# First-round maxima of the last layer one iteration earlier, and the second layer's values-times-weights product as three f32r products

## Time and profile before

| | us |
|---|---|
| median of 3 runs | 2929.89 (2924.7 to 2931.28) |
| the profiled execution | 2927.05 |
| its span, first to last instruction | 2924.9 |
| PE busy | 2673.6 (91%), at a mean granted clock of 0.916 |
| DVE busy | 1857.2 (63%) |
| ACT busy | 1210.1 (41%) |
| POOL busy | 270.2 (9%) |

### The profile page before, as it was taken

The page is one execution under the profiler, slowest core; times in us unless marked ns, Lnnn a source line. Parts: engine busy times, 40 slices in busy tenths (PEclk is TensorE's granted clock), DMA queues, the critical chain, the costliest instruction groups (busy, mean ns, idle before and its releaser), DMA issues.

```text
span 2924.9 us, 25567 instructions
## 1 busy us (share of the span) xinstructions
PE 2673.6 (91%) x9636; PEld 1380.7 (47%) x9636; DVE 1857.2 (63%) x1973; ACT 1210.1 (41%) x2073; POOL 270.2 (9%) x138
## 2 busy tenths in 40 slices
PE   7999978989999898998989999898998989997888
PEld 4446644445544455444554445444464445542333
DVE  4624137776377764776558763787628777387987
ACT  3233122626235352444525354252632626224548
POOL 0030210010101001020110201002020010200000
PEclk7999987989989898998989989898998989978889
DMA  2000010100201011010200102001020100211100
GB/s 85 1 0 0 1 44 0 44 1 19 54 1 44 1 40 33 1 44 1 72 1 1 44 1 72 0 1 44 1 72 0 35 10 12 47 44 44 44 1 29
DMA packets 29292, 72.09 MB, mean 25 GB/s; under 512 B 10224, under 2 KB 10416, under 8 KB 28912
## 3 DMA queue, kind: packets, MB, share of 16 engines
q1 hardware_dynamic: 29168, 70.45, 9.6%
HBM read 11.40 MB, written 8.39 MB: 7 GB/s over the span
## 4 chain that ended last, share of the span: by engine, by line
PE 74%; DVE 18%; ACT 4%; issue 2%; SPq 1%; DMA 0%; DVEq 0%; ACTq 0%
PE ps L748 15%; PE ps L601 12%; PE ps L634 11%; PE ps L911 7%; PE ps L620 7%; DVE ba_nmx L1277 6%; PE ps L833 6%; PE ps L609 5%; DVE fa_nmx L1277 3%; PE ps L690 2%; PE ps L819 2%; ACT prb L1130 2%; DVE bb_nmx L1277 1%; DVE accb L1439 1%; PE ps L830 1%
## 5 line engine op out<-in xcount | busy, mean ns | idle before, releaser
L1130 ACT ACTIVATE prb<-ps 128x512 f32<-128x512 f32 x896 | 483.5, 601 | 319.4 <-PE ps L634 279.4
L1277 DVE TENSOR_REDUCE ba_nmx<-ps 128x1 f32<-128x1024 f32 x448 | 529.9, 1216 | 96.8 <-PE ps L620 94.4
L620 PE MATMUL ps<-ks,qs 96*128 96x512 f32 x896 | 374.6, 524 | 84.4 <-DVE ba_nmx L1277 64.1
L748 PE MATMUL ps<-pr,h 128*128 128x512 f32 x896 | 421.3, 595 | 1.6 <-ACT tmp L1029 1.0
L1439 DVE TENSOR_TENSOR accb<-accb,prb 128x1024 f32<-128x1024 f32 x336 | 394.0, 1217 | 14.8 <-ACT prb L1130 14.2
L634 PE MATMUL ps<-qs,ks 97*128 97x512 f32 x896 | 354.4, 471 | 13.9 <-ACT prb L1130 13.3
L1001 ACT ACTIVATE pr<-ps 128x512 f32<-128x512 f32 x336 | 195.5, 596 | 396.0 <-PE ps L833 188.6
L620 PEld LDWEIGHTS ps<-ks,qs 96*128 96x128 f32 x896 | 182.3, 227 | 266.3 <-DVE ba_nmx L1277 185.6
L634 PEld LDWEIGHTS ps<-qs,ks 97*128 97x128 f32 x896 | 161.6, 194 | 266.0 <-ACT prb L1130 201.0
L911 PE MATMUL ps<-prb,vb 128*32 128x512 f32 x1792 | 241.2, 611 | 2.9 <-ACT prb L1130 2.2
L748 PEld LDWEIGHTS ps<-pr,h 128*128 128x128 f32 x896 | 168.8, 190 | 148.6 <-issue 134.7
(11 more groups left out here) (300 smaller groups left out, 3058.9 us busy)
## 6 DMA issues: line engine op xcount, KB each, us to landing
qs<-part SPq DMA_DIRECT2D x168, 128.0 KB, 2.4
ks<-part SPq DMA_DIRECT2D x168, 128.0 KB, 2.4
xm<-in_x SPq DMA_DIRECT2D x8, 1024.0 KB, 5.7
out<-prb SPq DMA_DIRECT2D x28, 256.0 KB, 2.1
q2k<-part SPq DMA_DIRECT2D x48, 128.0 KB, 2.4
w<-in_weights SPq DMA_DIRECT2D x1, 2592.0 KB, 8.7
out<-pr SPq DMA_DIRECT2D x4, 256.0 KB, 2.0
qs<-ba_nmx_r SPq DMA_DIRECT2D x56, 4.0 KB, 1.8
```

The costliest lines, as they stand in the source:

```text
L620: mm = pe.matmul(o.ps[:, bank + jc, :], queries[0:STACK, tile(it)], keys[0:STACK, cols(jc)], start=True, stop=True)
L748: mm = pe.matmul(o.ps[:, 2 + ch, :], o.v[:, jt, tile(ch)], o.pr[:, t % 4, :], start=jt == 0, stop=jt == NT - 1)
L1130: act.activation(weights3(o, s, g), o.ps[:, turn3[score_use(s, g) % 3], :], ACT.Exp)\
L1277: dve.tensor_reduce(o.nmx[:, head, it:it + 1], o.ps[:, bank:bank + 2, :], AX.XY, ALU.max, negate=True).then_inc(o.max_sb[n].sem, 1)
```

## The change

Two things change, and all tables of `ORDER` are replaced.

1. **The head of a back is longer.** On PE it now reaches to the last of the 32 tiles of the first round's maxima, on DVE to the cast of these maxima, on SyncE to the four DMAs that write them into the queries. So the iteration that finishes batch b also takes the first-round maxima of batch b+1; for batch 0 they stand at the end of "fronts", and "backs" no longer has those of batch 6.
2. **Layer 1's product of values and weights is three f32r products.** ACT writes the values rounded to f32r (`v_hi`), DVE the rest (`v_lo`). Behind each of the 16 exponentials ACT copies the weights, rounded, to `p_hi`; POOL subtracts to get `p_lo`; PE sums `v_hi p_hi + v_hi p_lo + v_lo p_hi`. `p_hi` and `p_lo` have three buffers each. The product now waits for POOL's `p_lo`, and three steps instead of two lie between the scores and it.

```diff
@@ ORDER: all fifteen tables are replaced
...
+            o.v_hi, o.v_lo = tokens(o.ql2), tokens(o.kh2)
+            o.p_hi = [o.kl2[:, 0, 0:IW], o.kl2[:, 0, IW:], o.kl2[:, 1, 0:IW]]
+            o.p_lo = [o.kl2[:, 1, IW:], o.qh2[:, 1, 0:IW], o.qh2[:, 1, IW:]]
...
@@ sync
                         yield from stacks(b, u)
+                        yield from shift_rows(b, u)
                         if u == 0:
                             yield "head"
-                        yield from shift_rows(b, u)
...
@@ gpsimd
+                def low_part(b, t):
+
+                    pool.wait_ge(o.p_hi_sb.sem, o.p_hi_sb.at(b, t + 1))
+                    pool.tensor_tensor(o.p_lo[t % 3], o.pr[:, t % 4, :], bf32(o.p_hi[t % 3]), ALU.subtract)\
+                        .then_inc(o.p_lo_sb.sem, 1)
...
                         for jg in range(4):
+                            for t in (2 * (4 * ic + jg), 2 * (4 * ic + jg) + 1):
+                                if n == 1:
+                                    low_part(b, t)
+                                    yield
                             add_pair(b, n, 4 * ic + jg)
...
@@ tensor
-                        pe.wait_ge(o.exped[n].sem, o.exped[n].at(b, t + 1))
+                        if n == 1:
+                            pe.wait_ge(o.p_lo_sb.sem, o.p_lo_sb.at(b, t + 1))
+                        else:
+                            pe.wait_ge(o.exped[n].sem, o.exped[n].at(b, t + 1))
...
+                            for values, weights in ((o.v_hi, o.p_hi), (o.v_hi, o.p_lo), (o.v_lo, o.p_hi)):
+                                mm = pe.matmul(o.ps[:, 2 + ch, :], values[:, jt, tile(ch)], weights[t % 3],
...
+                    behind = 3 if n == 1 else 2
...
-                        yield "head" if half else None
+                        yield
...
-                            yield
+                            yield "head" if u == 0 and k == QUAD * NT - 1 else None
...
@@ scalar
+                        if n == 1:
+                            act.wait_ge(o.exped[1].sem, o.exped[1].at(b, t + 1))
+                            if t >= 3:
+                                act.wait_ge(o.weighed[1].sem, o.weighed[1].at(b, t - 2))
+                            act.activation(o.p_hi[t % 3], o.pr[:, t % 4, :], ACT.Copy).then_inc(o.p_hi_sb.sem, 1)
+                            yield
...
@@ vector
-                    yield "head"
+                    yield
...
-                        yield
+                        yield None if u else "head"
```

More of the change, by code:

```diff
@@ L762, in chunks @@
                         yield
-                        if t > 1:
-                            weigh(t - 2)
+                        if t >= behind:
+                            weigh(t - behind)
                             yield
@@ L768, in chunks @@
                             yield
-                    for t in (STEPS - 2, STEPS - 1):
+                    for t in range(STEPS - behind, STEPS):
                         weigh(t)
@@ L1033, in chunks @@
                         yield
-                        if t == NT + 1:
+                        if n == 1:
[4 more added lines that the diff above has]
+                            yield
+                        if t == (NT + 2 if n == 1 else NT + 1):
                             take(0)
@@ L1088, in front @@
                     yield from to_stacks(b, 1, True)
-                    take_values(b, 1, 0, o.v, 2)
-                    yield
+                    for half in range(2):
+                        act.wait_ge(o.v_ps[1].sem, o.v_ps[1].at(b, half + 1))
+                        act.activation(o.v_hi[:, 4 * half:4 * half + 4, :].rearrange("p (k a) c -> p k a c", a=2),
+                                       o.ps[:, 2 - 2 * half:4 - 2 * half, :].rearrange("p k (a c) -> p k a c", a=2),
+                                       ACT.Copy).then_inc(o.v_hi_sb.sem, 1)
+                        yield
                     shift_row(b, 1, o.qs01, ROW)
@@ L1399, in front @@
                     yield from low_stacks(b, 1, True)
-                    take_values(b, 1, 1, o.v, 0)
-                    yield
+                    for half in range(2):
+                        dve.wait_ge(o.v_hi_sb.sem, o.v_hi_sb.at(b, half + 1))
+                        rows = slice(4 * half, 4 * half + 4)
+                        dve.tensor_tensor(o.v_lo[:, rows, :].rearrange("p (k a) c -> p k a c", a=2),
+                                          o.ps[:, 2 - 2 * half:4 - 2 * half, :].rearrange("p k (a c) -> p k a c", a=2),
+                                          bf32(o.v_hi[:, rows, :]).rearrange("p (k a) c -> p k a c", a=2), ALU.subtract)\
+                            .then_inc(o.v_sb[1][half].sem, 1)
+                        yield
                     yield from maxima(b, 1, 1)
```

40 lines of the change are left out of this document (25 added, 15 removed), and 48 rows, old and new, of the table ORDER.

## The result

The changed kernel takes 2853.26 us (median of 4 runs, 2852.63 to 2854.85) against 2929.23 us for the kernel before on the same chip: a ratio of 0.9744, 95% interval 0.9727 to 0.9760. Forecast were 2731 us, with a range of 2630 to 2835. The direction was right, but three fifths of the expected 198 us didn't come. The profiled execution took 2852.89 us with a span of 2851.1.

A forecast was written before the change was run, and what follows sets the result against it. Iterations were taken to alternate between PE waiting for DVE and pure PE bound. Four stretches sum to 319.5 us; 469.7 + 6 x 319.5 + 339.4 = 2726 us of span, 2731 us forecast, range 2630 to 2835.

The forecast's parts named there:

- fronts: Part ahead of the six iterations: 435.9 us plus 39.1 for 32 uncovered tiles less 5.3 for shorter products, 469.7 us.
- backs: Part after the six iterations, DVE bound: 378.5 us less 39.1 for the maxima it no longer has, 339.4 us.
- What bounds the kernel: Middle iteration: stretches where PE waits for DVE alternate with pure PE ones; 57 of 351.6 us lost and winnable.
- Part 1: Layer 1's three f32r products: 5.3 us less PE work per batch, 42 us in all, real only where PE bounds.
- B: Layer 1's chunks with second-round maxima: PE 42.4, DVE 46, POOL 40.5 us, coupled; 48 us, bounds 44 and 56.
- The subtraction: POOL's 16 subtractions per batch in layer 1's chunks: 1.27 us each, 20.3 us per batch.
- POOL and DVE: Layer 1's chunks: POOL's additions and subtractions can delay four DVE pieces with SBUF inputs; 4 us allowed, range 0 to 9.
- A: Middle, first 16 steps and layer 0: 88.5 us of PE work times 1.11, the like old stretch's factor; 98.5 us.
- C: Second 16 steps and layer 2's projections: 74.3 us of work with a 6.6 us stall; 86 us, bounds 80 and 92.
- D: Layer 2's chunks, next head and its first-round maxima: 84.1 us of PE work, 87 us with 3 for the seam.
- the overlap: Head's first tile: its wait for 24 stack DMAs just hidden by 18.7 us of PE work; no-overlap rival 0.08.
- POOL becomes the bound: Rival for layer 1's chunks: subtractions of 2.0 us or waiting for DVE stall PE; 2765 to 2805 us, chance 0.15.

The follow-up runs named there:

- m1: Changed kernel with DVE's maxima of layers 0 and 1 read over 64 of 1024 columns; 2787.7 us.
- s1: Changed kernel with DVE's 32 second-round maxima of the last layer read over 64 of 1024 columns; 2791.9 us.
- m3: Changed kernel with all maxima, both rounds, read over 64 of 1024 columns, PE's products kept; 2675.7 us.
- h1: Changed kernel with layer 1's product as one f32 product per block, without ACT's copies and POOL's subtractions; 2858.8 us.
- n1: Changed kernel without POOL's subtractions: three products kept, rounded weights used twice, low parts of the weights left out; 2857.0 us.
- h2: Changed kernel with layer 1's product in f32, no low parts, and second-round maxima read over 64 of 1024 columns; 2812.1 us.
- m2: Changed kernel with the score products of layer 0's and 1's maxima computed twice into the same banks; 2848.1 us.
- c2: Changed kernel with seven unused PE products ahead of group norm 2, in the middle iterations alone; 2845.2 us.
- o2: Changed kernel, middle iterations reordered: second-round tiles and first score steps earlier, layer 0's and 1's tiles of maxima spread between other steps; 2918.8 us.
- x2: Changed kernel with maxima from 64 of 1024 keys, other keys' products left out, and second-round stack DMAs issued by two engines; 2626.8 us.

## Why the prediction was right or wrong

- **What bounds the kernel: half right.** DVE holds the stretches with tiles (m1, s1), PE the last one. But the 57 us said to be lost rested on a count of PE's work that was too low. The step that failed is the count of PE's work: "Everything else is f32 at 0.43 per 512-column record or f32r at 0.23", pieces times their shortest starts; it holds 289.3 us where the records have 299.4. In the changed kernel a score product takes 0.24 us start to start among its like, and 0.34 behind a group of value products:

```profile
1516.17 1.06 PE L933 MATMUL ps<-prb,vb 128*32 128x512 f32 x8
1517.16 0.50 PE L646 MATMUL ps<-qs,ks 97*128 97x512 f32 x1
1517.50 0.40 PE L646 MATMUL ps<-q2k,ks 97*128 97x512 f32 x1
1517.74 0.40 PE L646 MATMUL ps<-qs,ks 97*128 97x512 f32 x1
```

  The records of the kernel before give 309 us of work, and this could be read when the prediction was made: busy time less half of what lay at the lower clock. An estimate from all records of the changed kernel's middle iteration generalises the example. At the pace that each kind of product keeps among its like they come to 281.5 us. Some 13 us lie at the 266 places where PE goes from one kind to another without a pause, 0.05 us each, and 4.7 at the 28 pauses, ahead of which a product shows its full length. In m3 it is 13 and 2.8 us. The prediction put the change of kinds at nothing but for 0.08 us per group of value products. Why PE needs longer there stays open.
- **Part 1, PE's work: right in size (5.4 us measured for 5.3), its worth left open.** The step said "42 us in all, real only where PE is the bound", and B was then reckoned with DVE's 46 us as its longest work beside PE's 42.4; how much of the 5.3 us was left by that it doesn't say. It is 1.0 us per iteration (h1) and 5.5 us in all. Part 1 alone in the old order wasn't tried.
- **The subtraction: right.** Forecast 1.27 us; 16 per batch, and their median is 1.290:

```profile
L547 POOL TENSOR_TENSOR q2k<-pr,q2k x112: 1264/1290/1734, 181.5 to 2317.8; 128x512 fp32r<-128x512 f32 x112
```

- **POOL and DVE: right.** 4 us were allowed in B, about 3.6 came: the two pieces of L1362 took 2.88 and 1.84 us instead of 0.745, and one of L1358 1.04 instead of 0.68. The first of them beside POOL's addition of 1634.03 to 1636.91:

```profile
1634.58 2.88 DVE L1362 SCALAR_TENSOR_TENSOR xm<-tmp,vec,xm 128x512 f32<-128x512 f32 x1
```

  It ends 0.55 us behind the addition, as in the earlier trace rows, and the reductions keep 1.21 us. POOL's addition took 2.88 us instead of 2.36 in turn. The section of the Trainium skill that the prediction weighed ("SBUF — State Buffer", "Who interferes with whom") has the two exclude each other and a reduction never take part; the trace agrees. But n1, without the subtractions, has no less of it: there the additions do it.
- **A: the factor 1.11 was two errors in one.** It was drawn from 88.0 us for 79.1 counted. In truth that stretch had 84.7 us of work, all at the full clock, and lost 3.3. A has 94.5 of work and loses 13.8, 7.6 of it to the clock. The sentence that failed is "this is in the factor, since the wait for the shift rows at its start is gone": in the stretch that gave the factor layer 1's tiles stood one at a time between score and value products, and PE waited for none of them. The sentence also has "9 us of DVE for 5 of PE"; at the prediction's own rate seven tiles are 3.2 us of PE. m1 prices both clusters at 11.1 us.
- **B: mechanism right, size off.** "Three engines nearly equal and coupled", 48 us for 51.8. PE's work was right (43.1 for 42.4), DVE was busy 42.5 us for 46; but 4.8 us go to the clock, 3.2 of them to its fall in the cluster ahead and 1.6 to the one at 1641.4, and 3.8 are idle. POOL's subtractions had no part in it (n1).
- **C: bounds held, value low.** 91.8 us for 86 (80 to 92). The stall was forecast as 6.6 us from the last reduction, and is 7.0; work was 3.2 us short. Before, PE's clock loss and idle time in that stretch were 8.5 us, now 14.3: 5.8 us of what A and B won are given back here.
- **D, "backs", the overlap: right; "fronts": right by luck.** D 87.6 for 87, its tiles cost PE their products alone; "backs" 340.0 for 339.4; the first tile of the head waits for no transfer. "Fronts" has 469.9 us for 469.7, but it was added up as 39.1 us for the tiles less 5.3 for the shorter product. By h1, which has 466.6 there, the tiles and the order cost 30.7 and the three products add 3.3: two errors of 8 us that cancel.
- **The rivals.** "POOL becomes the bound" would have given 2765 to 2805; subtractions of 1.29 us and n1 exclude it. None named what happened: losses that move from the stretch that is cleared to the seams behind it, together with a floor that was never as low as counted. The range ended at 2835, 18 us short, because both the factor and the floor came from one count, so that all cases shared its error. The listed chances add up to 1.02.

Summed up for the middle iteration, 20.0 us over the forecast: 10.1 us of the miss are PE's work, 3.8 the clusters in A beyond the factor, 3.1 B's clock and idle time, 2.6 C's seam, 0.4 D. Shown by runs are the price of the clusters (m1), DVE's hold on B (s1, h2), that GpSimd's subtractions don't hold B (n1), how little came back with the clock (m2, c2) and the transfers behind the clusters (o2, x2). That the count was short is shown by the records and by m3; where it was short is an estimate, and the 2.6 us of C's seam are read from the trace alone.

## What to carry to other kernels

Take an engine's work from its records (busy time, corrected for the clock), never from pieces times their shortest interval, or add a term for each change from one kind to another: an error of 5% in the floor was a quarter of the loss that was to be won. When a new order clears one stretch, ask of each seam behind it what arrives next and when: here a wait of 3 us to spare on 3 MB of transfers stood right behind the cluster. A saving on an engine that takes turns with another at nearly the same pace can be worth little, here about a fifth of itself; with the other's work gone (the maxima, in h2 and s1) some two thirds of it showed.

## What the hardware showed beyond that

- 24 transfers of 128 KB from SBUF to SBUF take 17.6 to 18.1 us from the first issue to the first product that reads them, whether one engine issues them or two.
- POOL's subtraction of 128x512 with an f32r output takes 1.290 us in the median, the f32 addition of that size in the same kernel (L542) 1.278, and the shortest of both 1.26: the output's type costs next to nothing.
- In the changed kernel's 1.2 GHz stretches, behind a cluster in which PE was idle 0.4 us in every 1.13, four products took 2.35 us; with the tiles computed twice in the same place (m2) the clock was 1.00 throughout A.
